# Feed-forward of a transformer layer: value tiles multiplied straight out of PSUM, and the Gelu of all gate tiles in one piece, one half-step earlier

## The reference, cut to what matters

```python
def ffn_layer(x, g, bln, W1, b1, W2, b2):
    mu = x.mean(-1, keepdims=True)
    var = ((x - mu) ** 2).mean(-1, keepdims=True)
    xn = (x - mu) / jnp.sqrt(var + 1e-05) * g + bln
    hg = xn @ W1 + b1                     # 128 -> 2 * 341
    a, gate = jnp.split(hg, 2, -1)        # values, gates
    return a * jax.nn.gelu(gate, approximate=False) @ W2 + b2
for i in range(DEPTH):                    # DEPTH = 6
    x = attn_layer(shift_tokens(x), Wqkv[i], q_scale[i], k_scale[i], Wo[i]) + x
    x = ffn_layer(shift_tokens(x), ln_g[i], ln_b[i], W1[i], b1[i], W2[i], b2[i]) + x
```

## Time and profile before

| | |
|---|---|
| median of 3 runs | 3550.07 us (3541.12 to 3565.05) |
| the profiled execution, first to last instruction (its span) | 3549.6 us |
| mean granted clock of TensorE | 0.963 of full speed |
| busy: TensorE matmul, weight load | 95%, 62% of the span |
| busy: VectorE, ScalarE, GpSimd | 66%, 67%, 33% |
| chain that ended last | TensorE 82%, ScalarE 6%, issue 5%, VectorE 5% |

### The profile page before, as it was taken

The page is one execution under the profiler, slowest core; times in us unless marked ns, Lnnn a source line. Parts: engine busy times, 40 slices in busy tenths (PEclk is TensorE's granted clock), DMA queues, the critical chain, the costliest instruction groups (busy, mean ns, idle before and its releaser), DMA issues.

```text
span 3549.6 us, 59598 instructions
## 1 busy us (share of the span) xinstructions
PE 3381.0 (95%) x18480; PEld 2208.0 (62%) x18480; DVE 2360.0 (66%) x4059; ACT 2372.3 (67%) x4353; POOL 1167.2 (33%) x1073
## 2 busy tenths in 40 slices
PE   6898898999999999999999999999999999999997
PEld 3565556666666666666666666666666666666664
DVE  5565566667667666766766676676667667666763
ACT  3343346777777667776776777777767777767873
POOL 2000003333444233533334533335433345333330
PEclk9898898999999999999999999999999999999997
DMA  2000001010111001110001111011100011100100
GB/s 71 1 0 0 0 0 37 36 37 36 49 38 45 33 31 40 49 46 32 36 33 42 49 41 36 31 39 48 48 32 37 35 42 51 39 35 33 38 34 21
DMA packets 101752, 122.63 MB, mean 35 GB/s; under 512 B 21972, under 2 KB 50770, under 8 KB 101458
## 3 DMA queue, kind: packets, MB, share of 16 engines
q1 hardware_dynamic: 101586, 121.09, 9.8%
HBM read 19.32 MB, written 1.05 MB: 6 GB/s over the span
## 4 chain that ended last, share of the span: by engine, by line
PE 82%; ACT 6%; issue 5%; DVE 5%; POOL 0%; DMA 0%; DVEq 0%; SPq 0%; ACTq 0%; POOLq 0%
PE bank L712 13%; PE bank L734 11%; PE bank L532 5%; PE bank L605 5%; PE bank L751 5%; PE bank L690 5%; PE bank L710 4%; PE bank L658 4%; PE bank L688 4%; PE bank L534 4%; PE bank L533 4%; PE bank L720 4%; PE bank L700 3%; PE bank L580 2%; PE bank L659 2%
## 5 line engine op out<-in xcount | busy, mean ns | idle before, releaser
L473 POOL TENSOR_TENSOR sq_lo<-sq_q,sq_hi 128x512 fp32r<-128x512 f32 x192 | 244.7, 1275 | 1621.5 <-ACT sq_hi L908 1621.5
L712 PE MATMUL bank<-fin 64*128 64x160 f32 (+1 forms) x3072 | 605.4, 317 | 0.0
L1193 DVE TENSOR_REDUCE neg_max<-bank 128x2 bf16<-128x320 f32 x768 | 357.2, 488 | 270.2 <-PE bank L690 266.3
L734 PEld LDWEIGHTS bank<-probs_t,v_sb 128*128 128x128 f32 x3072 | 466.0, 198 | 72.5 <-issue 33.1
L712 PEld LDWEIGHTS bank<-fin 64*128 64x128 f32 x3072 | 438.5, 187 | 109.0 <-issue 3.4
L734 PE MATMUL bank<-probs_t,v_sb 128*128 128x160 f32 (+1 forms) x3072 | 503.2, 309 | 0.7 <-ACT probs_t L932 0.7
L923 ACT ACTIVATE neg_row<-bank 1x512 bf16<-1x512 f32 x384 | 225.3, 587 | 275.9 <-PE bank L700 271.1
L932 ACT ACTIVATE probs_t<-bank 128x320 f32<-128x320 f32 (+1 forms) x768 | 284.1, 422 | 181.2 <-PE bank L720 181.2
L482 POOL TENSOR_TENSOR rot_k<-tc_k,ts_k 128x512 f32<-128x512 f32 x192 | 260.6, 1357 | 363.4 <-issue 363.3
L1203 DVE TENSOR_TENSOR o_feat<-bank,inv_sums 64x512 f32<-64x512 f32 x384 | 263.5, 686 | 153.8 <-ACT inv_sums L944 150.4
L482 POOL TENSOR_TENSOR rot_q<-tc_q,ts_q 128x512 f32<-128x512 f32 x192 | 245.1, 1277 | 293.5 <-DMA ts_q<-sr_q 271.4
(11 more groups left out here) (154 smaller groups left out, 6407.5 us busy)
## 6 DMA issues: line engine op xcount, KB each, us to landing
ts_q<-sr_q SPq DMA_DIRECT2D x384, 128.0 KB, 2.1
ts_k<-sr_k SPq DMA_DIRECT2D x384, 128.0 KB, 2.1
w_raw<-in_L_ffn_Wqkv SPq DMA_DIRECT2D x48, 192.0 KB, 2.7
wo_sb<-in_L_ffn_Wo SPq DMA_DIRECT2D x6, 512.0 KB, 3.7
w_raw<-in_L_ffn_W SPq DMA_DIRECT2D x6, 341.0 KB, 3.1
rot_sb<-in_rotary SPq DMA_DIRECT2D x1, 1024.0 KB
out<-x_tok SPq DMA_DIRECT2D x16, 64.0 KB, 1.6
w_sb<-in_L_ffn_W SPq DMA_DIRECT2D x6, 128.0 KB
```

The lines of the kernel that those rows point to most:

```text
L473: pool.tensor_tensor(sq_lo[:, i, :], sq[i][:], sq_hi[:, i, :].bitcast(F32), ALU.subtract).then_inc(s_sql[i], 1)
L712: pe.matmul(dst[:, at:at + q], k_fin[rows, p % 2, c * P:(c + 1) * P], q_fin[rows, p % 2, c * P:c * P + q], start=False, stop=False)
L734: mm = pe.matmul(dst[:, c * P:c * P + q], v_sb[:, c, p, h * DIM_HEAD:h * DIM_HEAD + P], probs_t[:, h, c * KEYS:c * KEYS + q], start=(c == ...
L1193: dve.tensor_reduce(neg_max[:, h, 2 * b:2 * b + 2], bank[2 + 2 * h + b][:, 0:2 * KEYS].rearrange("p (c k) -> p c k", c=2), AX_X, ALU.max, ...
```

## The change

On TensorE the three value tiles move one or two slots later, to (4, 1), (5, -1) and (5, 1). ScalarE's two pieces of Gelu become one piece in slot (4, 0), ahead of `max_row(n, 1)` of step 4. VectorE no longer writes the value tiles to SBUF: once Gelu is through, it reads each value tile from bank 7, adds the bias and multiplies by the gate tile in one operation, into `gates`. Its `product` and the semaphore `f_prod` are gone; `down` waits for the count of tiles. The buffer `values` is gone; the weights of the first stage that lay in it get a small buffer.

```diff
-        values = sb("values", [P, NF, TOK])
+        wkqv_place = sb("wkqv_place", [P, 3 * P])
-        wkqv_sb = values[:, 0, 0:3 * P]
+        wkqv_sb = wkqv_place[:, :]
...
                 def down():
-                    pe.wait_ge(f_prod, f + 1)
+                    pe.wait_ge(f_he, 2 * NF * (f + 1))
...
-                        (4, 0): up(3), (4, 1): up(4), (5, -1): up(5), (6, 0): down}
+                        (4, 1): up(3), (5, -1): up(4), (5, 1): up(5), (6, 0): down}
...
                     act.preload_act_table(ACT.Gelu)
                     act.wait_ge(f_he, 2 * NF * f + NF)
                     act.activation(gates[:, 0:NF - 1, :], gates[:, 0:NF - 1, :], ACT.Gelu)
-
-                def gelu_rest():
                     n = FFN_TILES[-1][1]
                     act.activation(gates[0:n, NF - 1, :], gates[0:n, NF - 1, :], ACT.Gelu).then_inc(f_gelu, 1)
                     act.preload_act_table_set(LN_EXP)
-                return {(1, 0): square_f, (1, 1): rstd_f_, (4, 1): gelu, (5, -1): gelu_rest}
+                return {(1, 0): square_f, (1, 1): rstd_f_, (4, 0): gelu}
...
-                def up(i):
+                def gate(i):
                     def run():
-                        n = FFN_TILES[i % NF][1]
+                        n = FFN_TILES[i][1]
                         dve.wait_ge(f_h, 2 * NF * f + i + 1)
-                        dst = (gates if i < NF else values)[0:n, i % NF, :]
-                        dve.tensor_scalar(dst, bank[7][0:n, :], b1_sb[0:n, i, bass.ds(l, 1)], None, ALU.add
+                        dve.tensor_scalar(gates[0:n, i, :], bank[7][0:n, :], b1_sb[0:n, i, bass.ds(l, 1)], None, ALU.add
                                           ).then_inc(f_he, 1)
                     return run
-                def product():
-                    n = FFN_TILES[-1][1]
-                    dve.wait_ge(f_gelu, f + 1)
-                    dve.wait_ge(f_he, 2 * NF * (f + 1))
-                    dve.tensor_tensor(gates[:, 0:NF - 1, :], gates[:, 0:NF - 1, :], values[:, 0:NF - 1, :], ALU.mult)
-                    dve.tensor_tensor(gates[0:n, NF - 1, :], gates[0:n, NF - 1, :], values[0:n, NF - 1, :], ALU.mult
-                                      ).then_inc(f_prod, 1)
+                def value(i):
+                    def run():
+                        n = FFN_TILES[i][1]
+                        dve.wait_ge(f_gelu, f + 1)
+                        dve.wait_ge(f_h, 2 * NF * f + NF + i + 1)
+                        dve.scalar_tensor_tensor(out=gates[0:n, i, :], in0=bank[7][0:n, :],
+                                                 scalar=b1_sb[0:n, NF + i, bass.ds(l, 1)], in1=gates[0:n, i, :],
+                                                 op0=ALU.add, op1=ALU.mult).then_inc(f_he, 1)
+                    return run
...
-                return {(0, 0): mid, (1, 0): centre, (2, 0): norm, (2, 1): up(0), (3, 0): up(1), (3, 1): up(2),
-                        (4, 0): up(3), (4, 1): up(4), (5, -1): up(5), (5, 1): product, (6, 0): residual}
+                return {(0, 0): mid, (1, 0): centre, (2, 0): norm, (2, 1): gate(0), (3, 0): gate(1), (3, 1): gate(2),
+                        (4, 1): value(0), (5, -1): value(1), (5, 1): value(2), (6, 0): residual}
```

More of the change, by code:

```diff
@@ L301, in build_program @@
         f_gelu = sem("f_gelu")
-        f_prod = sem("f_prod")
         f_w2 = sem("f_w2")
```

## The result

The changed kernel takes 3617.77 us (median of 4 runs, 3610.9 to 3623.84) against 3552.95 us for the kernel before in the same series (4 runs, 3541.12 to 3565.05): ratio 1.0175, 95% interval 1.0138 to 1.0211. It is slower by 65 us where 31 were forecast, and its time lies 3 us above the range. The profiled execution has a span of 3612.6 us, 63.0 more than that of before.

The account below looks back on a forecast made before the run. TensorE, busy 95% of the span, was taken as the bound, losing time only by waits or low clock. Moved Gelu +31.3, last feed-forward -1.9, clock +2 gave +31.4 us on 3549.6: 3581, range 3542 to 3615.

Parts of the forecast that it names:

- The moved Gelu: Step 4: a 4.19 us block makes TensorE wait 3.14 for the row of maxima; net of the old wait, +31.3 us.
- The old wait disappears wholly, since in step 5 ScalarE then does what it does in step 3: Step 5: TensorE's wait for the row of maxima, 1.78 us per body, goes in all 23 bodies.
- What is late next: VectorE's `o_feat` and value tiles behind the later row in step 4: cover holds by 0.6 us; otherwise 4 to 17, taken 0.
- the last part: List of expected signs: L720 waits about 3.1 us 23 times, none in step 5; count of `o_feat` waits unchanged.
- The clock: TensorE's clock behind the wait costs 2.3 us per body against 2.2 now, +2; bounds 31 us back to 65 more.
- rival A: Clock takes more: low stretch behind the longer wait one stage longer, 1.68 us more per body, 3620; chance 0.17.
- The VectorE part: Three new operations for three old and the product's going: worth 0 in the 23 bodies, bounds 0 and 44 us gain.
- In the last feed-forward: Done alone at the end, the product lies on the path, so its going gives -1.9 us.
- B: Not slower: behind L720 of step 4 the clock gives back what the wait costs, -31 us; 3548, chance 0.13.
- C: Faster: ScalarE reaches or does the Gelu block so much sooner that TensorE hardly waits; 3460, chance 0.06.
- D: Table switches cost more at the new place, each load waiting out an operation, 2.1 us per body; 3630, chance 0.04.
- the page on table loads: Skill page: 1283 ns per load plus about 1380 ns drain, making the block 6.95 us and the sum 63 larger; rejected.

Follow-up runs that it names:

- Experiment 1: The changed kernel with value tile 1 taken behind `o_feat` on VectorE in step 5: 3585.09 us, ratio 1.0089 to the kernel before.
- experiment 2: The kernel before with only the Gelu moved, in one piece in slot (4, 0); tiles, values buffer and product as they were: 3650.66 us, ratio 1.026.
- experiment 3: The changed kernel with value tile 0 back in slot (4, 0) on TensorE, in front of the wait; VectorE unchanged: 3677.09 us, ratio 1.034.
- experiment 4: The changed kernel with value 1 behind `o_feat` on VectorE and value tile 0 back in slot (4, 0) on TensorE: 3652.64 us, ratio 1.0283.
- experiment 5: The changed kernel without the two table loads and with Exp computed in place of Gelu, a measure and no variant: 3506.51 us, ratio 0.9858.
- experiment 9: New tile operation without product, Gelu in its old pieces and places, and step 5's row of maxima copied by VectorE: 3550.44 us, ratio 0.9974 to the kernel before.
- experiment 10: The kernel of experiment 9 with TensorE's norm of k ahead of `max_scores` of head 1 in step 5: 3490.98 us, ratio 0.9808.
- experiment 11: The kernel of experiment 10 with TensorE's value tile 1 also ahead of `max_scores` of head 1 in step 5: 3476.3 us, ratio 0.977.
- experiment 6: The changed kernel's new tile operation without product, but Gelu in its old place and the value tiles later: 3639.89 us, ratio 1.0247 to the kernel before.
- experiment 7: The kernel before with step 5's row of maxima copied by VectorE: 3547.2 us, ratio 0.9964; with value tile 2 also behind `o_feat`: 3569.14 us, ratio 1.0045.

## Why the prediction was wrong

**The moved Gelu: right.** 4.19 for the block, 3.08 of wait where the working gave 3.14 from start to start, 23 times, and no wait at L719 of step 5: +33.6 us by the rows of waits, against +31.3.

**"The old wait disappears wholly, since in step 5 ScalarE then does what it does in step 3": the step that failed.** It is true of ScalarE and was not asked of VectorE. A tile stood in slot (5, -1) ahead of `o_feat` before, too, and `o_feat` was late; TensorE was then still waiting for the row of maxima. With that cover gone 0.66 is left in each body with a feed-forward, and the waits for `o_feat` are 14.1 us more in all. The paragraph "What is late next" looked only at step 4 and said of value 1 that it could be emptied "at leisure", and the last part said that the count of waits for `o_feat` stays. It did price a late VectorE, at 4 to 17 us, and took 0. Experiment 1 removes the wait by the order alone, experiment 2 has it with the old operations. Experiment 1 also gives the size of the miss: without these waits the ratio is 1.0089, and the forecast's is 3581 / 3550.07 = 1.0087. So near a hit holds some luck, as the clock's share of that difference is only in part explained.

**The clock: right in kind, mis-sized.** 2.3 us per body were taken, 67.1 / 23 = 2.9 were measured: 17.8 us more than before by the windows, 23.7 by the busy time, and not 2; this is the largest single part of the 31.6 us by which the span was missed. (Of the 6 us between the two measures the change is hardly the cause: in the first 700 us, where it does nothing, the clock is low for 119 us after and 106 before, and half of that counts.) (The windows of before had been read as 12 at 0.86 and 9 at 0.72; the 9 are 0.72 to 0.75, 49.3 us in place of 50.4.) It lies inside the stated bounds, about a third of the way to rival A (1.68 more per body). The reason given for taking so little, dense matmuls behind the wait, was sound as far as it went: experiments 3 and 4 show falls two to three times as long without the tile there. But they show it as a brake on a larger loss, and not as a saving against before.

**The VectorE part: 0 came out, by a reason that holds for the old place alone.** TensorE waits for maxima 3.4 us before and 3.6 after, so the product's going gave nothing back there, as said. That at its new time it meets GpSimd (experiment 2: 31.7 us of waits for maxima) was not seen: the bounds of 0 and 44 us knew only of its duration of 1.9 and nothing of the 1.78 that half of it takes there. In the last feed-forward -1.7 came for -1.9.

**The rivals.** A named the right sign and, by chance of two causes, nearly the time (3620). B fell: the clock gave nothing back. C, at 3460, has its measure in experiment 5: without the loads, 3506. D and the page on table loads: L957 starts 0.02 behind the Exp before it and ends 0.02 before the Gelu, at the new place as at the old. The Trainium skill's 1283 ns (ScalarE: Activation LUTs, "What ACT_TABLE_LOAD costs") agree with the 1.28 of the rows, its drain of 1380 ns does not show.

The range ended 3 us too low. It had no term for the wait for `o_feat`, and it left out the far half of A, which is where the clock's cost together with that wait came to lie.

What stays open: what exactly lets the clock come back. A wait's length decides in experiments 9 to 11, but 0.73 in step 6 of experiment 6 brought falls in 15 of 22 bodies, and 0.71 in experiment 7 in 6 of 23; the work behind it decides in experiments 3 and 4. Bodies of one kernel with the same wait and the same work fall differently (3.4 to 20 us in experiment 3). No run separates what kind of matmul counts.

## What to carry to other kernels

When a wait disappears, ask at its old place of every engine, not only of the one that was waited for, what it was doing under that cover: here VectorE's order (14 us of waits) and, in the kernel with the product, its meeting with GpSimd (28 us). Where TensorE is the bound, a wait costs more than its length through the clock: with the loads gone 65.5 us less of it gave 106 of span (experiment 5); shortening one from 1.35 to 0.89, by moving work that exists in front of it, made the 23 bodies 40 us faster, of which 10 are waiting (experiments 9 and 10). An operation may be cheap only at the time at which it stands: cost a moved operation beside its new neighbours.

## What the runs showed of the hardware that was not expected

- Some VectorE operations with all operands in SBUF slow down beside GpSimd's: the 85-row product 1.78 in place of 0.68, a scalar_tensor_tensor 1.68 in place of 0.68, a rounding copy 1.38 in place of 0.43. Either side can be the one held up: L473 of GpSimd started 0.03 to 0.06 ahead of the product in 18 bodies of experiment 2; in 17 the product took 1.78, in one it kept 0.68 and L473 took 1.84 in place of 1.28. Of the changed kernel's 72 operations that take a value tile from PSUM none took over 752 ns.
- The clock stayed at its low level (1.2 GHz) for up to 20 us behind a wait of 2.38 while TensorE was busy 100% of the window (22.00 of 22.00 in experiment 3), and for 3.4 us in 5 other bodies of the same kernel.
- Behind a wait of 0.18 it never fell in 23 bodies, behind 0.89 twice, behind 1.35 18 times, behind 1.62 21 times, behind 2.38 and 3.08 each time. At other places 0.73 brought it down in 15 of 22.
